# Layer 0's mixture of experts: six experts on gathered slots between dense chunks of two

## What is computed

```python
def _L0_cond_ref(x, subjects, weights):          # x as (128, 32, 256), one 32x32 matrix for each subject
    return jnp.einsum('bct,bcd->bdt', x, weights[subjects])

def _L0_ffn_ref(x, Wr, Wg, Wu, Wd):              # E = 8 experts, H = 256, I = 176, cap = 320
    xf = x.reshape(N, H)
    gate = jax.nn.softmax(jnp.einsum('nh,eh->ne', xf, Wr), axis=-1)
    top2_val, top2_idx = jax.lax.top_k(gate, 2)
    flat_idx = jnp.concatenate([top2_idx[:, 0], top2_idx[:, 1]])
    flat_val = jnp.concatenate([top2_val[:, 0], top2_val[:, 1]])
    onehot = jax.nn.one_hot(flat_idx, E, dtype=jnp.int32)
    rank = (jnp.cumsum(onehot, axis=0) * onehot).sum(-1)
    w_assign = jnp.where(rank <= cap, flat_val, 0.0)
    comb = jnp.zeros((N, E), x.dtype).at[jnp.tile(jnp.arange(N), 2), flat_idx].add(w_assign)
    g = jax.nn.silu(jnp.einsum('nh,eih->eni', xf, Wg))
    out_e = jnp.einsum('eni,ehi->enh', g * jnp.einsum('nh,eih->eni', xf, Wu), Wd)
    return jnp.einsum('ne,enh->nh', comb, out_e)

x = x + _L0_ffn_ref(_L0_cond_ref(x, ...), ...)
x = x + _L1_ffn_ref(_L1_cond_ref(x, ...), ...)
```

## Time and profile before

| what | us |
|---|---|
| median of 3 runs (418.45 to 420.94) | 418.47 |
| span of the profiled execution | 449.4 |
| TensorE busy in it | 409.6 |
| VectorE, ScalarE, GpSimd busy | 235.8, 151.3, 172.2 |

### The profile page before, as it was taken

One profiled execution on the slowest core, in us unless ns is written; L12 is line 12 of the kernel. 1 busy time (PEld: TensorE's weight loads), 2 busy tenths in 40 slices (PEclk: granted clock), 3 DMA queues, 4 the chain that ended last, 5 costly groups with the idle time before them and its releaser, 6 DMA issues.

```text
span 449.4 us, 6240 instructions
## 1 busy us (share of the span) xinstructions
PE 409.6 (91%) x1978; PEld 340.2 (76%) x1978; DVE 235.8 (52%) x516; ACT 151.3 (34%) x308; POOL 172.2 (38%) x157
## 2 busy tenths in 40 slices
PE   1999999999899999999999995969978898799996
PEld 1877888888688888888787784967867787699875
DVE  6966445545954122211488763744534444466557
ACT  2545333333453443233346261421211212122140
POOL 3510311311225544344321177056656655444400
PEclk9999999999999999999999998899869988899999
DMA  7402443234703233311111686022223223211175
GB/s 227 165 5 59 152 127 119 83 117 141 247 13 118 104 120 117 117 36 35 35 37 55 169 187 186 26 72 84 81 70 95 82 72 78 75 49 61 65 272 214
DMA packets 17208, 46.79 MB, mean 104 GB/s; under 512 B 3466, under 2 KB 6050, under 8 KB 16874
## 3 DMA queue, kind: packets, MB, share of 16 engines
q1 hardware_dynamic: 12666, 34.07, 24.0%
q0 software_dynamic: 4512, 12.33, 9.2%
HBM read 38.10 MB, written 8.29 MB: 103 GB/s over the span
## 4 chain that ended last, share of the span: by engine, by line
PE 82%; DVE 8%; another core or an unknown queue 4%; issue 3%; ACT 2%; DMA 1%; SPq 0%; DVEq 0%; ACTq 0%
PE gu L1192 12%; PE gu L1194 12%; PE gu L1193 11%; PE y L1478 10%; PE y L1192 4%; PE y L1194 4%; PE y L1193 4%; PE gu L1458 4%; PE gu L1462 4%; PE gu L1459 4%; PE gu L1411 2%; PE gu L1470 2%; PE y L1555 2%; PE gu L1391 1%
## 5 line engine op out<-in xcount | busy, mean ns | idle before, releaser
L483 POOL TENSOR_TENSOR w_lo<-w_raw,w_hi 128x512 fp32r<-128x512 f32 (+3 forms) x44 | 52.8, 1220 | 145.9 <-ACT w_hi L552 131.4
L1192 PE MATMUL gu<-act_hi,w_hi 128*128 128x512 f32 x196 | 78.4, 400 | 0.7 <-DVE hid L823 0.7
L1194 PE MATMUL gu<-act_hi,w_lo 128*128 128x512 f32 x196 | 77.0, 393 | 0.0
L1193 PE MATMUL gu<-act_lo,w_hi 128*128 128x512 f32 x196 | 76.8, 392 | 0.0
L526 POOL DMA_INDIRECT y_k<-w_raw,put x47 | 46.2, 983 | 60.2 <-DVE w_raw L1111 51.9
L576 ACT ACTIVATE hid_hi<-hid 128x512 fp32r<-128x512 f32 x46 | 29.0, 632 | 89.5 <-DVE hid L823 48.0
L1458 PE MATMUL gu<-w_hi,xgT 128*128 x94 | 37.3, 398 | 20.9 <-issue 12.1
L1478 PE MATMUL y<-w_dn,t_hidT 88*128 x188 | 54.3, 416 | 1.4 <-DVE t_hidT L1118 1.3
L823 DVE TENSOR_TENSOR hid<-silu,gu 128x512 f32<-128x512 f32 x24 | 16.5, 687 | 65.7 <-PE gu L1194 61.2
L709 ACT ACTIVATE silu<-gu 128x176 f32<-128x176 f32 x47 | 14.9, 317 | 102.7 <-PE gu L1462 76.1
L836 DVE TENSOR_TENSOR hid_lo<-hid,hid_hi 128x512 fp32r<-128x512 f32 x46 | 31.7, 692 | 27.2 <-ACT hid_hi L576 26.3
(11 more groups left out here) (229 smaller groups left out, 714.7 us busy)
## 6 DMA issues: line engine op xcount, KB each, us to landing
w_raw<-in_w_gu SPq DMA_DIRECT2D x16, 352.0 KB, 4.3
w_raw<-in_wc SPq DMA_DIRECT2D x8, 576.0 KB, 3.9
w_raw<-in_w SPq DMA_DIRECT2D x11, 384.0 KB, 3.1
w_raw<-y_k SPq DMA_DIRECT2D x5, 512.0 KB, 6.3
w_raw<-scr SPq DMA_DIRECT2D x8, 256.0 KB, 4.3
w_dn<-in_w_dn SPq DMA_DIRECT2D x1, 1936.0 KB
w_raw<-in_ws SPq DMA_DIRECT2D x5, 384.0 KB, 3.4
w_dn<-y_k SPq DMA_DIRECT2D x3, 512.0 KB, 9.3
```

The lines of the kernel that those rows point to most:

```text
L483: nc.gpsimd.tensor_tensor(w_lo[par][:, w], w_raw[par][:, w], w_hi[par][:, w].bitcast(F32), ALU.subtract).then_inc(split, 1)
L1192: T.matmul(out, w[0], x[0], start=start, stop=False)
L1193: T.matmul(out, w[0], x[1], start=False, stop=False)
L1194: return T.matmul(out, w[1], x[0], start=False, stop=stop)
```

## The change

Layer 0's experts 0 and 1 stay dense: their 2 x 128 first rows are chunks 0 and 1, and their remaining 48 rows each share chunk 2 (padded to 64 each). The experts 2 to 7 work on 320 slots each. Two experts form a pair of 640 slots, five tiles of 128 of which the middle one is shared.

- Front: TensorE also forms the conditioned x by rows (`x_by_rows`), ScalarE copies it to SBUF, SP writes it to `x2`. `ranks` moves ahead of the gate/up of chunk 0; VectorE makes slots from the ranks and one-hots as layer 1 does; the tables `row_e`, `tile_e`, `planes` are made by GpSimd at the start and not by VectorE in COND. `slots0` runs before chunk 1. The combine columns of experts 0 and 1 are spread by matmul with the identity (16 matmuls); the HBM route (`scr`, `combs`) and `sel` are gone.
- SP's queue: `cst1`, the weights of experts 2 and 3 (368 KB and 256 KB each), a clear of 2 MB of `y_k` with zeros, the 1 MB of `x2`, then `small`, `xT`, COND's first chunk, the weights of experts 4 to 7, chunk 2's; after all scatters the eight reads of `y_k` (256 KB each), then COND's second chunk.
- GpSimd: splits the weights of experts 2 and 3, clears the pads of the hidden tiles, issues ten gathers (experts 2 to 5), then for each expert its two or three scatters, with the gathers of expert 6 behind the scatters of expert 2 and those of expert 7 behind the scatters of expert 3.
- TensorE, for each sparse expert: 18 matmuls of 320 columns (`q_gate_up`), the turns of the next expert's tiles (`q_turn_in`), then the down product of the expert before (`q_down`), which has no split parts: 6 float32 matmuls of 256 columns.
- End: the down products of chunks 0 to 2 and the gate/up of chunk 2 follow the sparse experts. The rows read back are weighed by ScalarE and GpSimd (first choice) and VectorE (second choice, sum), and TensorE adds them transposed to `Y` (`add_rows`, 16 float32 matmuls).

The core of the diff:

```diff
-NC = {L0: E0 * I_EXP // P, COND: I_COND // P, SH: -(-I_SH // P)}
+NC = {L0: ED + 1, COND: I_COND // P, SH: -(-I_SH // P)}
...
+            sp.dma_start(cst1[:], d["cst1"]).then_inc(s_in["cst1"], 16)
+            for q in range(2):
+                q_gate_up(q)
+                q_down(q)
+            sp.wait_ge(s_zero, 1)
+            sp.dma_start(d["y_k"][0:N * K0].rearrange("(p r) h -> p r h", p=P),
+                         zeros.unsqueeze(1).broadcast_to([P, N * K0 // P, H])).then_inc(s_cleared, 16)
+            sp.wait_ge(s_x0c, 4)
+            sp.dma_start(d["x2"].rearrange("(t p) h -> p t h", p=P), x_rows).then_inc(s_x0, 16)
...
+            for p in range(ES // 2):
+                sp.wait_ge(q_st[p], 16 * PAIR_TILES)
+            for t in range(NT):
+                sp.dma_start(q_y[t], d["y_k"][0:N * K0].rearrange("(n k) h -> n k h", k=K0)[t * P:(t + 1) * P]
+                             ).then_inc(s_fin[t], 16)
...
+            pool.wait_ge(s_x0, 16)
+            pool.wait_ge(q_get, 1)
+            for q in range(ES - 2):
+                gathers0(q)
+            pool.wait_ge(s_cleared, 16)
+            pool.wait_ge(q_put, 1)
+            for q in range(ES):
+                scatters0(q)
+                if q < 2:
+                    gathers0(q + ES - 2)
...
             logits(logit_ps, 0, SM_R0, E0)
+            x_by_rows()
+            ranks()
             pe.wait_ge(s_actl, KH)
             gate_up(L0, 0, 0, 0)
             pe.wait_ge(s_actl, 2 * KH)
             pe.wait_ge(s_rlg, 1)
-            gate_up(L0, 0, 0, 1, between=ranks)
-            comb_transposed()
+            gate_up(L0, 0, 0, 1, between=lambda: pe.wait_ge(s_rkr, 1))
+            slots0()
             gate_up(L0, 1, 1, 0)
+            comb_spread()
+            q_turn_in(0)
             gate_up(L0, 1, 1, 1)
-            comb_spread()
-            gate_up(L0, 2, 0, 0)
...
+            for q in range(ES):
+                q_gate_up(q)
+                if q + 1 < ES:
+                    q_turn_in(q + 1)
+                if q:
+                    q_down(q - 1)
+            q_down(ES - 1)
+            pe.wait_ge(q_o1, ES // 2)
+            pe.wait_ge(q_o2, ES)
+            pe.wait_ge(q_hid, 2 * ES)
+            for s in range(2):
+                down(L0, 0, 0, s, start=True)
+            for s in range(2):
+                gate_up(L0, ED, 0, s)
+            for c in range(1, ED + 1):
                 for s in range(2):
-                    down(L0, c, c, s, start=c == 0)
...
+                    down(L0, c, c % 2, s)
+            add_rows()
```

In a sparse expert the other engines do this for each gate/up result:

```diff
+            def q_silu(q):
+                act.wait_ge(q_gu, 3 * q + 1)
+                if q:
+                    act.wait_ge(q_hid, 2 * q)
+                A.activation(q_siluA, q_gu_ps[0], ACT.Silu).then_inc(q_act, 1)
+                act.wait_ge(q_gu, 3 * q + 3)
+                A.activation(q_siluC[REST_AT:REST_AT + I_REST], q_gu_ps[2][0:I_REST], ACT.Silu).then_inc(q_act, 1)
...
+            for q in range(ES):
+                q_silu(q)
+                if q + 1 < ES:
+                    q_turned(q + 1)
+                if q:
+                    q_rows(q - 1)
+                if q + 2 < ES:
+                    q_round(q + 2)
```

More of the change, by code:

```diff
@@ L890, in _ @@
+            for s in range(2):
+                hid_low(4 + s, s)
+            for t in range(NT):
+                dve.wait_ge(*((q_wp, t // 2 + 1) if t % 2 else (q_wa, t // 2 + 1)))
+                V.scalar_tensor_tensor(out=q_y[t][:, 0], in0=q_y[t][:, 1], scalar=r_w[:, t, 1:2], in1=q_y[t][:, 0],
+                                       op0=ALU.mult, op1=ALU.add).then_inc(q_sum, 1)
             dve.wait_ge(s_in["xT"], 16)
             for s in range(2):
-                dve.wait_ge(s_d, 2 * C0[COND] - 1 + s)
+                dve.wait_ge(s_y0, s + 1)
@@ L1222, in _, with x_by_rows @@
             eye = cst[:, CS_ID:CS_ID + P]
-            def comb_transposed():
-                pe.wait_ge(s_cmb, 1)
+            def x_by_rows():
+                pe.wait_ge(s_actf, 2 * KH)
+                for t in range(NT):
+                    last = T.matmul(row_ps[t // 2][:, t % 2 * H:(t % 2 + 1) * H], wblk[:, t].rearrange("p b d -> p (b d)"),
+                                    x_tok[:, t], start=True, stop=True)
+                    if t % 2:
+                        last.then_inc(s_x0t, 1)
@@ new lines, in q_turn_in @@
+            def q_turn_in(q):
+                p, at = q // 2 * PAIR_TILES, q % 2 * (SHARED_AT + 1)
+                if q == 0:
+                    pe.wait_ge(s_sprS, 2)
+                tiles_of = [(p + at + n, q_two[:, :, n * P:(n + 1) * P]) for n in range(2)]
+                if not at:
+                    tiles_of.append((p + SHARED_AT, q_one))
+                pe.wait_ge(q_in[q], 16 * len(tiles_of))
+                for i, out in tiles_of:
+                    for k in range(KH):
+                        last = T.transpose(out[:, k], q_xg[i % Q_XG][:, k * P:(k + 1) * P], eye)
+                last.then_inc(q_turn, 1)
@@ new lines, in q_down, with product @@
+            def q_down(q):
+                b, of = q % 2, q_dn[q % 3]
+                rest = slice(REST_AT, REST_AT + I_REST)
+                pe.wait_ge(q_hid, 2 * q + 2)
+                pe.wait_ge(q_dw[q % 3], 16 * (q // 3 + 1))
+                if q:
+                    pe.wait_ge(q_o2, q)
+                else:
+                    pe.wait_ge(s_sprS, 4)
+                if b == 0 and q:
+                    pe.wait_ge(q_o1, q // 2)
+                def product(ps, at, start, stop):
+                    T.matmul(ps, q_hA[b][:, at:at + P], of[:, 0:H], start=start, stop=False)
+                    return T.matmul(ps, q_hC[b][rest, at:at + P], of[rest, H:2 * H], start=False, stop=stop)
+                if b:
+                    product(q_out1_ps, 0, False, True).then_inc(q_dn1, 1)
+                for n in range(2):
+                    last = product(q_out2_ps[:, n * H:(n + 1) * H], (b + n) * P, True, True)
+                if not b:
+                    last = product(q_out1_ps, 2 * P, True, False)
+                last.then_inc(q_dn2, 1)
@@ L1231, in comb_spread @@
-            def comb_spread():
-                pe.wait_ge(s_sel, 1)
-                for c in range(SPREAD):
-                    for s in range(2):
-                        pe.wait_ge(s_cmbS, s + 1)
-                        if c == 1:
-                            pe.wait_ge(s_cmbF, s + 1)
-                        T.matmul(Y[c][s][:], sel[0:CB_N, c * P:(c + 1) * P], combT_r[0:CB_N, half(s)], start=True,
-                                 stop=True).then_inc(s_sprd, 1)
+                        last.then_inc(s_y0, 1)
```

466 lines of the change are left out of this document (356 added, 110 removed).

## The result

The changed kernel takes 424.73 us (median of 4 executions, 421.74 to 428.17), the kernel before 418.60 beside it (418.45 to 420.94): 1.0109 of it, 95% interval 1.007 to 1.0147. In this set it is slower by about 1%, where 1.8% faster was forecast. The profiled execution took 424.74 us, its span is 422.5 us and its mean granted clock 0.956.

The account below looks back on a forecast made before the run. TensorE was taken to bound layer 0's dense experts. Removing 66.3 us of chunks and adding 13.3 (front), 40.9 (sparse) and 4.5 gave 7.6 us less: 418.47 to 410.9 us, range 401 to 420.

Parts of the forecast that it names:

- the mark: Start of COND's second-half LoRA matmuls, the program being the same from there on; forecast to move from 120.97 to 113.4 us.
- The front: Everything up to the first sparse matmul (x by rows, ranks, slots, chunks 0 and 1, column spread): 48.4 us.
- collisions: In the front, GpSimd's splits and clears slow VectorE's chain to the one-hots: 2 us taken, between 0 and 5.3.
- late x: Rival: x rows land at 47 us or later behind the 2 MB clear on SP's queue; 424 us, chance 0.09.
- The sparse experts: Experts 2 to 7 at 5.8 us each, plus an open chain, last down and gather waits: 40.9 us, ending at 89.3.
- expert 3's open chain: Silu, tile copy and subtraction ahead of expert 3's gate/up, with no down product yet to cover them: 1.8 us.
- GpSimd's gathers: Gathers for experts 6 and 7 queue behind scatters, so TensorE waits about 1.5 us each: 3 us taken.
- latency rival: Sparse experts wait for turn, copy, subtraction and gather as layer 1 does, plus one half-clock stretch: 416.9 us, chance 0.20.
- The end: Hand-over and dense rest to 105.0 us, y_k reads hidden, row additions to 107.1, hand-over to COND 6.3: 113.4.
- The step from profile to time: The 7.6 us gain, found in a 449.4 us profile, is subtracted unscaled from the unprofiled median of 418.47 us.
- cover holds better: Rival: no collision (-2), GpSimd ahead as unprofiled (-3), reads early (-1): 405 us, chance 0.25.
- slower: Rival: x rows land late behind the clear on SP's queue, 11 us behind get, with a clock drop: 424 us, chance 0.09.

Follow-up runs that it names:

- the splits later: Changed kernel, but GpSimd splits weights of experts 2 and 3 and clears pads behind VectorE's one-hots: 419.1 us, 0.9941 of the kernel before; on the 453 us chip 458.1 us.
- all three edits: Changed kernel with second down products on all 128 rows, all gathers before the first scatter, and GpSimd's splits and clears behind the one-hots: 402.1 us, 0.9546 of the kernel before.
- the grouped order: Changed kernel with each sparse expert's three down products on 128 rows first, then the three on 48 rows: 413.5 us, 0.9878 of the kernel before.
- the full-rows run: Changed kernel, second product of each sparse down group on all 128 rows: 452.6 us on the 453.3 us chip (the 3.19 us wait); 410.9 us on a 419.95 us chip.

## Why the prediction was wrong

**The remainder behind the mark** is the same in both kernels, as the prediction had it: 291.6 and 291.9 us with half clock taken off. That 296.7 and 297.0 us were measured for the pair is in part luck, since each lost 5.1 us there; other executions of the changed kernel and its variants lose 0 to 1.7.

**The front** was right in sum. 48.4 was forecast for the first sparse matmul, with 2 us of collisions in it; it came at 46.98. The collision was dearer than the 2 us taken (inside the bounds of 0 to 5.3): from the ranks to the last of the one-hots VectorE took 9.1 us (24.30 to 33.39), with the splits later 4.9 (26.71 to 31.65). Up to 3.4 us of half clock were not in the sum either. What made up for it: the ranks came 0.9 us earlier, and slots0 took 1.05 us where 3.01 had been taken from products of 96 columns; these have 32. So that the front came out right is errors that cancel, in part by luck. Rows of x were in time, as costed: GpSimd waited for get alone, and the "late x" rival didn't happen.

**The sparse experts** hold the first step that failed. "Down is 6 unsplit matmuls of 256 columns; [...] 0.43 each: 2.6 us" took its pace from the tile loop. There all down matmuls have 88 rows from row 0; here every second one has 48 rows from row 64 on, behind one on 128, and a product takes 0.63 us. The row's duration was read without asking what stood before it. 36 products x 0.2 us = 7.2 us. The other terms of this part hold: gate/up 0.147 us a matmul, expert 3's open chain 1.47 us idle (1.8 forecast), GpSimd's gathers 2.1 us (3 forecast). With slow products, gather wait and half clock gone the six experts take 36.8 us (all three edits); the same sum, 36.9 and 1.0 for the last down, was 37.9.

**The clock** is the second step that failed, and the larger. The sum has every matmul at full clock; half clock stood in the text only as a side of the latency rival, with one stretch and 2.5 us. Stage by stage, with half the length of every half-clock stretch taken off (an estimate, and an upper bound, as TensorE waits in a part of them):

| us | forecast | measured | lost to the clock | at full clock |
|---|---|---|---|---|
| front, to the first sparse matmul | 48.4 | 47.0 | 3.4 | 43.6 |
| sparse experts | 40.9 | 52.2 | 7.1 | 45.1 |
| dense rest | 15.7 | 18.0 | 3.2 | 14.8 |
| rows added, to the mark | 8.4 | 8.6 | 0 | 8.6 |
| mark | 113.4 | 125.8 | 13.7 | 112.2 |

The kernel before, on a chip of 419 us, has its mark at 122.4 and lost 1.7 ahead of it: 120.7 at full clock. So at full clock the changed kernel is 8.5 us earlier, close to the 7.6 forecast, and that, too, is partly luck, since 7.2 us of slow products are offset by a front costed 5 us too dear. What turned the gain into a loss is 12 us more at half clock. In the changed kernel's other profile, with its mark at 122.15, it is 10.2 us lost against 1.7, and the two kernels come out even.

What made the clock fall is shown in part. The stretch at the end of the sparse experts comes with the alternating down products, seven profiles against five, and the grouped order takes it away without a change of the work. So the term of the sum that was mis-sized by 7 us brought this stretch along. The stretch in the front comes with the wait of 2.9 us that the collision makes. The stretch from 71.4 us on is open: it followed the wait ahead of expert 6's turns in three profiles of seven. Why load gaps of 0.33 us should lower the clock is not shown by any run. The Trainium skill (TensorE: Matmul & The Clock Gate, "A second HAM failure mode: psum-queue depth-cycling") describes a clock that swings in a bf16 kernel that cycles through PSUM banks, because the engine idles a little between groups of matmuls. The stretch at the last down products would agree, if the 0.33 us gaps of the loads are such idling, which the trace can't show in the array itself. The section cited in the prediction, on waits, fits the front and the full-rows run with its 3.19 us better than this stretch.

**The end** was right: 15.7 us of dense rest forecast, 15.5 at full clock (18.0 in after, 6.3 us of them at half clock). From the first row addition to the mark 8.6 against 8.4. The reads of y_k are hidden.

**Sum of the miss at the mark, profile after:** front -1.4, sparse +11.3, dense rest +2.3, end +0.2: +12.4, and 113.4 + 12.4 = 125.8. The 11.3 are 7.2 of slow products, about 7 of half clock (10.2 us from 71.4, and 3.9 from 95.3 to 99.2, halved), less 0.9 at GpSimd and the 1.1 by which the sum was too high; the product term and the clock term overlap by about 1.

**The step from profile to time** held, but not for its reason. It took the absolute difference of the marks over to another median, on the ground that the 31 us between profile and median lie in the tile loop. They do, 27.7 of 30.0 us, but they belong to another chip and not to the profiler. With that falls the reason given for the "cover holds better" rival, that the stalls are partly the profiler's.

**The rivals.** The latency rival named the right symptom (half clock) with the wrong cause: apart from expert 3's 1.47 us, no expert waited for its turn and copy chain. The "slower" rival's 424 is next to the measured 424.7 by chance: x was in time. By its own rates, 219 GB/s for the first 3.9 MB and 120 for the other 3, x would also land near 44 and not at 47. 424.7 is above the whole range, since no case had more than one stretch at half clock, nor a pace for the down products other than 0.43.

## What to carry to other kernels

Before taking the pace of a matmul from another loop, look at what alternates with it: here products on 128 rows and on rows 64 to 111 in turn cost 0.63 us each, in groups 0.48, and on equal rows, padded with zeros, 0.43. Where TensorE's share is high and the stage is still long, read the granted clock beside it and look for gaps in the weight loads. Before calling a part of two profiles equal or different, take the time at half clock off both. And compare a profile's span with the times of its own kernel before using its stalls: 7% apart was another chip here, whose stalls at indirect DMAs the timed runs did not have.

## What the hardware showed

- A change between 128 rows and 48 rows from row 64 on, between float32 matmuls of 256 columns, costs 0.2 us, with a 0.33 us gap ahead of the weight load. A change from 128 rows to 88 rows from row 0 on shows no such gap.
- Seven of seven profiles with such changes at every down product have 6.8 to 10.2 us at half clock that begin at the last two down groups; five of five without them have none there.
- The granted clock of one program differs from execution to execution: 0.956 to 0.988 in ten, with 426.0 to 413.6 us.
- Chips differ by 8% on the kernel before (453.3 against 419.0 us), and ScalarE stands idle 2 to 4 us at a time with its work ready while GpSimd issues gathers. Fifteen gathers in a row made the changed kernel 2.7% slower than the kernel before there, and gained 5.5 us elsewhere (4.3 by the means). What differs in the chip is open.
- A VectorE instruction on 16 elements a partition took 2.75 us beside GpSimd's subtraction and clears, 0.18 without them.
